# A gated state-space block with a ternary feed-forward: two convolutions moved from VectorE to TensorE, weight sums and step sizes rescheduled, and the first row of the tail in halves

## The reference, cut to what matters

```python
xi = in_proj_w @ ctx.T                      # 512 channels x 512 times
u  = silu(conv4(xi) + conv_b)               # depthwise, causal, 4 taps
dt_lo, Bm, Cm = split(x_proj_w @ u)         # 16, 16, 16 rows
delta = softplus(dt_proj_w @ dt_lo + dt_b)  # 512 x 512
state = state * exp(delta * A) + delta * u * B    # 16 states, scanned over time
y = sum_n(state * C) + D * u
y = y * silu(layernorm(x))                  # gate
x = x + tanh(g_xattn) * y.T
# then, on rows of x: ternary feed-forward
# s = mean|w|; wq = round(tanh(w / s)) * arctanh(s)      for w1, w2, w3 (2048 x 512)
# linear(v, w) = int8_round(rmsnorm(v)) @ wq
out = x + tanh(g_ffn) * linear(silu(linear(n, w1)) * linear(n, w2), w3),   n = layernorm(x)
```

## Time and profile before

| | us |
|---|---|
| median of 3 runs | 691.34 (689.88 to 695.04) |
| the profiled execution: its time | 689.91 |
| the profiled execution: its span | 687.9 |
| mean granted clock of PE | 0.928 |
| busy: PE / DVE / ACT / POOL | 605.1 / 609.2 / 557.1 / 550.8 |

### The profile page before, as it was taken

One profiled execution on the slowest core, in us unless ns is written; L12 is line 12 of the kernel. 1 busy time (PEld: TensorE's weight loads), 2 busy tenths in 40 slices (PEclk: granted clock), 3 DMA queues, 4 the chain that ended last, 5 costly groups with the idle time before them and its releaser, 6 DMA issues.

```text
span 687.9 us, 8231 instructions
## 1 busy us (share of the span) xinstructions
PE 605.1 (88%) x2538; PEld 247.5 (36%) x2538; DVE 609.2 (89%) x582; ACT 557.1 (81%) x804; POOL 550.8 (80%) x341
## 2 busy tenths in 40 slices
PE   6994657999788999999999999978898989787997
PEld 3430121445344343423333433332333333333443
DVE  4788889998897899999999999999999999977764
ACT  3648986588979998998989998989889878757883
POOL 5135548886987999999989999998999999978641
PEclk9857886999999999999999999999999999898999
DMA  7958963464953222215402212154212121000000
GB/s 206 331 149 275 331 220 122 135 201 134 281 204 89 46 62 54 84 48 126 100 24 61 49 53 55 50 123 108 62 46 55 38 55 40 15 16 0 22 28 30
DMA packets 40379, 70.97 MB, mean 103 GB/s; under 512 B 10848, under 2 KB 13408, under 8 KB 38288
## 3 DMA queue, kind: packets, MB, share of 16 engines
q1 hardware_dynamic: 32320, 48.44, 25.5%
q10 hardware_dynamic: 8016, 22.02, 9.5%
HBM read 49.46 MB, written 4.46 MB: 78 GB/s over the span
## 4 chain that ended last, share of the span: by engine, by line
PE 28%; DVE 23%; issue 7%; ACT 7%; POOL 4%; DVEq 0%; ACTq 0%; POOLq 0%
DVE hb L1201 14%; PE ring L1581 9%; DVE dbu_ps L1192 5%; PE y_ps L1559 5%; PE ring L1686 4%; PE du_ps L1546 3%; PE ring L1527 2%; POOL h L655 2%; ACT dA L918 2%; PE ring L1649 2%; DVE am L1260 1%; PE ring L1508 1%; PE ring L1641 1%; DVE h_max L1339 1%; POOL hb L712 1%
## 5 line engine op out<-in xcount | busy, mean ns | idle before, releaser
L1201 DVE TENSOR_TENSOR_SCAN hb<-dA,dbu_ps 128x1024 f32<-128x1024 f32 x128 | 292.1, 2282 | 11.0 <-ACT dA L918 4.3
L712 POOL TENSOR_TENSOR hb<-hb,bc_rep 128x2048 f32<-128x2048 f32 x52 | 236.0, 4539 | 38.4 <-DVE hb L1201 35.8
L1192 DVE TENSOR_TENSOR dbu_ps<-du_ps,bc_rep 128x1024 f32<-128x1024 f32 x128 | 157.8, 1233 | 19.5 <-PE du_ps L1546 10.5
L918 ACT ACTIVATE dA<-dl_rep,a_neg 128x511 f32<-128x511 f32 x252 | 160.8, 714 | 5.6 <-DVE hb L1201 3.5
L1559 PE MATMUL y_ps<-hb,sel_q 128*32 128x512 f32 x512 | 125.4, 635 | 1.3 <-POOL hb L712 1.2
L1546 PE MATMUL du_ps<-du,sel_q 32*128 32x512 f32 x128 | 77.1, 684 | 47.5 <-DVE dbu_ps L1192 44.5
L655 POOL TENSOR_TENSOR h<-h,up_sb 128x1024 f32<-128x1024 f32 x24 | 57.2, 2382 | 11.6 <-ACT up_sb L936 11.2
L1686 PE MATMUL ring<-w3T,hT 128*128 128x512 fp8e4 x256 | 61.2, 386 | 0.9 <-ACT hT L1007 0.5
L1559 PEld LDWEIGHTS y_ps<-hb,sel_q 128*32 128x32 f32 x512 | 28.6, 116 | 85.8 <-issue 81.8
L648 POOL TENSOR_TENSOR up_sb<-h,g3b 128x1024 f32<-128x1024 f32 x24 | 56.6, 2357 | 1.9
L1581 PE MATMUL ring<-w1T,a12T 128*128 128x512 fp8e4 x208 | 55.1, 389 | 1.2 <-ACT a12T L984 1.1
(11 more groups left out here) (182 smaller groups left out, 970.6 us busy)
## 6 DMA issues: line engine op xcount, KB each, us to landing
dl_rep<-delta SPq DMA_DIRECT2D x252, 64.0 KB, 2.0
bc_rep<-bc_scratch SPq DMA_DIRECT2D x28, 256.0 KB, 4.8
h<-in_L_ffn_w_dram ACTq DMA_DIRECT2D x7, 1024.0 KB, 5.8
x<-in_L_ffn_w_dram ACTq DMA_DIRECT2D x7, 1024.0 KB, 5.4
up_sb<-in_L_ffn_w_dram ACTq DMA_DIRECT2D x7, 1024.0 KB, 5.9
xt<-in_x_dram SPq DMA_DIRECT2D x16, 256.0 KB, 3.1
out_dram<-x SPq DMA_DIRECT2D x16, 256.0 KB, 2.0
x<-in_x_dram SPq DMA_DIRECT2D x2, 1024.0 KB, 8.2
```

The costliest lines, as they stand in the source:

```text
L712: g.tensor_tensor(hb[:, s % 4, :, :], hb[:, s % 4, :, :], c_rep(s // 16), ALU.mult)\
L918: ins = a.activation(dA[:, s % 2, i, 1:L], dl[:, 1:L], ACT.Exp, scale=a_neg[:, s % 16, i:i + 1])
L1192: v.tensor_tensor(dbu_ps[:, :, :], du_ps[:, :].unsqueeze(1).to_broadcast([P, 2, L]), b_rep(b)[:, 2 * half:2 * half + 2, :], ALU.mult).then ...
L1201: v.tensor_tensor_scan(hb[:, s % 4, 2 * half:2 * half + 2, :].rearrange("p a l -> p (a l)"), dA[:, s % 2, 2 * half:2 * half + 2, :].rearra ...
```

## The change

- The convolutions of tiles 4 and 5 go from DVE (steps 2 and 3) to PE, in step 1; ACT evacuates them in step 2. `tap` becomes a plain copy for them.
- The absolute sums of chunks 0 to 2 stand between the first `exps` of ACT, those of the chunks 3 to 11 in the steps 1 to 6. `exps(2)` stands ahead of ACT's loop. The refills are issued by SP (`next_chunk`) and not by ACT.
- The step sizes of step 0 are spread by DMA (`bcast_delta(0)`); L1621 goes. The load of the last z rows goes behind that of chunk 2.
- Three of the `z_row_stats` go ahead of step 0, and five stay, in the steps 4 to 8.
- `weight_scales` is split: `weight_sums` stays, the scales come after the second `add_input` of step 7, read the PSUM bank and have one instruction less.
- Tail: the row tile 12 is centred and gained by DVE in two halves (w1's row, w2's row), each with its own scale, quantisation, transpose and evacuation; PE gets ROW_FILL = 8 filling matmuls there. The statistics of rows 14 and 15 come later. The last states are summed in finer pieces. In row 15 all gains are on DVE, in three pieces, the sum of squares is in three, and LAST_FILL goes from 20 to 12.

```diff
-LAST_FILL = 20
+LAST_FILL = 12
+ROW_FILL = 8
...
 def late_convs(k):
+    if k == 0:
+        return [ET, AHEAD]
...
 def abs_chunks(s):
-    first = (0, 2, 4, 6, 8, 10, WCH)
-    return range(first[s], first[s + 1]) if s + 1 < len(first) else []
+    first = (3, 3, 4, 6, 7, 9, 10, WCH)
+    return range(first[s], first[s + 1]) if 0 <= s < len(first) - 1 else []
...  (SP)
-            for b in range(B):
+            for b in range(B - 1):
+                load_z(b)
...
+            def next_chunk(c):
+                sp.wait_ge(w_abs, c + 1)
+                load_chunk(c + WB)
...
             store_bc(0)
+            bcast_delta(0)
             bcast_delta(1)
             load_c(0)
             load_chunk(2)
+            load_z(B - 1)
...
+                    if s == 2:
+                        next_chunk(1)
+                    if s == 3:
+                        next_chunk(2)
+                    for c in abs_chunks(s - 2):
+                        next_chunk(c)
                     if s + 2 < Q * KQ:
                         bcast_delta(s + 2)
+                    if s == 1:
+                        next_chunk(0)
...  (POOL, after the loop)
-            row_rstd(TAIL)
-            row_rstd(TAIL + 1)
+            first_tail_powers()
             pool.wait_ge(a_tail, 2)
             times_up(TAIL - 1, 1)
-            row_rstd(TAIL + 2)
+            row_rstd(TAIL + 1)
             h_gain(TAIL - 1, 1)
-            row_rstd(TAIL + 3)
             hidden_rms(TAIL - 1)
             mul_gains(TAIL + 1)
+            row_rstd(TAIL + 2)
+            row_rstd(TAIL + 3)
...  (ACT)
+            def abs_sum(c):
+                act.wait_ge(*chunk_ld(c))
+                a.activation(chunk_buf(c), chunk_buf(c), ACT.Abs, accum_out=wsum[:, c:c + 1]).then_inc(w_abs, 1)
             exps(0)
             exps(1)
+            abs_sum(0)
             ctx_evac(1)
+            abs_sum(1)
+            exps(2)
             tap(ET)
+            abs_sum(2)
...
-                    elif 0 < s < Q * KQ - 1:
+                    elif 1 < s < Q * KQ - 1:
                         exps(s + 1)
...
+                    if q == (1 if k else 2):
                         for m in late_convs(k):
                             conv_evac(m)
...
                     for c in abs_chunks(s):
-                        act.wait_ge(*chunk_ld(c))
-                        a.activation(chunk_buf(c), chunk_buf(c), ACT.Abs, accum_out=wsum[:, c:c + 1])\
-                         .then_inc(w_abs, 1)
-                        act.wait_ge(w_abs, c + 1)
-                        a.dma_start(chunk_buf(c + WB), chunk_src((c + WB) % WCH)).then_inc(chunk_ld(c + WB)[0], 16)
+                        abs_sum(c)
...
-            square_sum(TAIL - 1, 0)
             quant(TAIL)
+            evac_first_aT(0)
+            evac_first_aT(1)
             normalise(TAIL + 1)
-            evac_aT(TAIL)
             square_sum(TAIL - 1, 1)
...  (DVE)
             copy_b(0)
+            z_row_stats(KQ // 2)
             copy_b(1)
+            z_row_stats(KQ // 2 + 1)
+            z_row_stats(KQ // 2 + 2)
...
+            def centred_gain(i):
+                v.scalar_tensor_tensor(a12[:, i, :], x1[:, (TAIL // ET) % XB, 0, :], fmv[:, TAIL % 4, 0:1],
+                                       (g2b if i else g1b)[:, :], ALU.subtract, ALU.mult).then_inc(a_tail, 1)
...
+            def weight_scales():
                 filled(dve, ("wsum", 0))
-                v.tensor_scalar(wm[:, :], bank(("wsum", 0))[:, 0:3], 1.0 / (H * D), None, ALU.mult).then_inc(w_mean, 1)
-                dve.wait_ge(w_mean, 1)
-                link(v.tensor_scalar(at[:, 0, :], wm[:, :], RMS_EPS, None, ALU.add))
-                link(v.tensor_scalar(at[:, 1, :], at[:, 0, :], 2 * ARTANH_HALF, None, ALU.mult))
+                total, mean = bank(("wsum", 0))[:, 0:3], 1.0 / (H * D)
+                v.tensor_scalar(wm[:, :], total, mean, None, ALU.mult).then_inc(w_mean, 1)
+                artanh = 2 * ARTANH_HALF
+                link(v.tensor_scalar(at[:, 1, :], total, artanh * mean, artanh * RMS_EPS, ALU.mult, ALU.add))
                 v.reciprocal(w_inv[:, :], at[:, 1, :]).then_inc(w_inv_done, 1)
-                link(v.tensor_scalar(at[:, 2, :], wm[:, :], -1.0, 1.0, ALU.mult, ALU.add))
+                link(v.tensor_scalar(at[:, 2, :], total, -mean, 1.0, ALU.mult, ALU.add))
                 link(v.reciprocal(at[:, 3, :], at[:, 2, :]))
-                v.scalar_tensor_tensor(at[:, 5, :], wm[:, :], 1.0, at[:, 3, :], ALU.add, ALU.mult).then_inc(w_scale, 1)
+                v.scalar_tensor_tensor(at[:, 5, :], total, float(H * D), at[:, 3, :], ALU.add, ALU.mult).then_inc(w_scale, 1)
...
                     add_input(s, 0)
-                    if k in (1, 2):
-                        z_row_stats(KQ // 2 + ET * (k - 1) + q)
-                    if k == 0 and q >= 2:
-                        convolve(ET + q - 2)
+                    if Q <= s < Q + 5:
+                        z_row_stats(KQ // 2 + 3 + s - Q)
                     if s == TERN_AT:
-                        weight_scales()
+                        weight_sums()
...
+                    if s == TERN_AT:
+                        weight_scales()
                     scan(s, 1)
...  (DVE, after the last scan)
             rows(TAIL)
-            row_bias(TAIL)
+            centred_gain(0)
+            first_tail_scale(0)
+            centred_gain(1)
+            first_tail_scale(1)
+            first_tail_dequant()
             rows(TAIL + 1)
-            tail_gains()
-            quant_scales(TAIL)
-            dequant_scales(TAIL)
+            hidden_max(TAIL - 1, 0)
             row_bias(TAIL + 1)
-            for ft in range(TAIL + 2, NT):
-                rows(ft)
-                row_bias(ft)
             for ft in range(TAIL, NT):
+                if ft == TAIL:
+                    mul_up(ft, 0)
                 hidden_row_scales(ft - 1)
-                mul_up(ft, 0)
+                if ft == TAIL:
+                    for late in (TAIL + 2, TAIL + 3):
+                        rows(late)
+                else:
+                    mul_up(ft, 0)
                 mul_up(ft, 1)
...
+                if ft == NT - 1:
+                    last_gain(0, 1024)
                 mul_up(ft, 2)
                 evac_hT(ft - 1)
...
+                if ft == NT - 1:
+                    last_gain(1024, 1536)
+                    hidden_max(ft, 0)
                 mul_up(ft, 3)
                 if ft == NT - 1:
-                    last_gain()
-                hidden_max(ft, 0)
+                    last_gain(1536, H)
+                else:
+                    hidden_max(ft, 0)
...  (PE, ahead of the loop)
-            pe.wait_ge(masks, 7)
-            pe.wait_ge(delta_done, 1)
-            mm(y_ps[:, :], sel_q[0:32, :], delta[0:32, 0, :], start=True, stop=True).then_inc(dl_bc, 1)
             bcast_du(0)
```

More of the change, by code:

```diff
@@ L1074, in _ @@
                             for c in range(4):
-                                if k == KQ - 1 and c == 3:
-                                    normalise(TAIL)
+                                if k == KQ - 1 and c == 2:
+                                    square_sum(TAIL - 1, 0)
                                 gate_silu(f, c)
@@ L1096, in _ @@
                 gate_silu(ft, 0)
[L1097 removed]
+                if TAIL < ft < NT - 2:
                     normalise(ft + 2)
@@ L1454, in _ @@
                     dequant_scales(ft + 1)
+                if ft == NT - 1:
+                    last_gain(0, 1024)
                 mul_up(ft, 2)
                 evac_hT(ft - 1)
+                if ft == TAIL:
+                    for late in (TAIL + 2, TAIL + 3):
+                        row_bias(late)
+                if ft == NT - 1:
+                    last_gain(1024, 1536)
+                    hidden_max(ft, 0)
                 mul_up(ft, 3)
                 if ft == NT - 1:
-                    last_gain()
-                hidden_max(ft, 0)
+                    last_gain(1536, H)
+                else:
+                    hidden_max(ft, 0)
                 if ft < NT - 1:
@@ L1561, in sum_states, with last_sums, state @@
                 ins.then_inc(sum_done, 1)
+            def last_sums():
+                s = Q * KQ - 1
+                def state(step, i):
+                    lo = 32 * (step % Q)
+                    return mm(y_ps[lo:lo + 32, :], sel_q[:, 0:32], hb[:, step % 4, i, :], start=False, stop=(i == NH - 1))
+                pe.wait_ge(hc_done, s)
+                state(s - 1, 0)
+                state(s - 1, 1)
+                pe.wait_ge(hc_first, 1)
+                for i in range(2):
+                    state(s, i)
+                    state(s - 1, 2 + i)
+                pe.wait_ge(hc_last, 1)
+                state(s, 2)
+                pe.wait_ge(hc_last, 2)
+                state(s, 3).then_inc(sum_done, 1)
             def skip_term(k):
@@ L1733, in _ @@
                     if q == 3:
+                        if f == 0:
```

(14 more changed lines are left out.)

158 lines of the change are left out of this document (97 added, 61 removed).

## The result

In the comparison made with the prediction, the changed kernel took 683.12 us (median of 4, 681.96 to 686.62), the kernel before 693.19 (4, 689.88 to 695.33): a ratio of 0.9889, interval 0.9855 to 0.9923. It is faster by a little over 1%, where 674.7 was forecast, in a range of 669 to 683: the median lies just above the range. Two later comparisons on other chips gave 682.88 against 690.84 (0.9902) and 684.62 against 693.06 (0.9895).

The account below looks back on a forecast made before the run. DVE's scans were taken as the backbone, with ACT bounding the head and PE's order the end. Gains of 14.0 (head), 0.8 (row 12) and 1.8 (row 15) sum to 16.6: span 671.3, median 674.7, range 669 to 683.

Parts of the forecast that it names:

- Rival A: Head: PE's convolutions run at the low clock, step 3 starts at 64.5, head gives 8; 681; chance 9%.
- rival B: Steps 8 to 19: late POOL or second-round loads hold PE's transposes, losing 4 to 8; 679 to 683; chance 14%.
- the head: Everything up to step 8: ACT's sums end at 92.8, step 8 begins at 100.2, 13.4 earlier.
- The tail: Behind the last scan: row 12 gains 0.8 and row 15 gains 1.8.
- The middle: Behind step 8: steps 9 to 11 save 1.6 in statistics, POOL's late product of step 7 costs 1.0.
- the wait is free: SP's refills ahead of each step's `bcast_delta`: waiting for a sum costs nothing while landings of up to 6.5 fit.
- Rival C: Step sizes queue behind chunk loads, `exps` of steps 3 to 9 late, about 4 a step; 700, slower; chance 4%.
- The start: Step 0: step sizes by DMA land near 32.2, `bcast_du(0)` ends sooner, step 0 begins at 33.2, 1.8 earlier.
- The scales: `weight_scales` before step 8: 7.4 where it was 11.9, with PE's sum over partitions hidden behind a scan.
- The port argument: Scales: DVE instructions with two SBUF inputs and POOL's exclude each other; reading PSUM shrinks those of 2.28 and 1.86.
- Row 12: Tail, row tile 12 in halves: `gate_up` starts near 621.7, `down(11)` at 635.1; gain 0.8, bounds -1 and 3.
- Row 15: Tail, last row tile: scales 1.1 earlier, 12 filling matmuls instead of 20; gain 1.8, bounds 1 and 2.5.

Follow-up runs that it names:

- the one with quarters: Kernel before, with each of the twelve second-round loads of weights cut to a quarter of its bytes; measured once, 685.98.
- the sizes first: Changed kernel with the step sizes of step 2 issued ahead of the loads of chunk 2 and the last z rows; 683.12 us.
- the z rows early: Changed kernel with the last batch's z rows loaded at the start, as before the change; 679.75 us, ratio to before 0.9841.
- all three: Changed kernel with z rows loaded at the start, row 12 as before, and step 2's step sizes ahead of chunk 2; 679.54 us, ratio 0.9817.

## Why the prediction was wrong

*Forecast 16.6 less; the medians differ by 8.0 to 10.1 in three comparisons.* Rival A had 681 and B 679 to 683, so the number alone would point near them. The table splits it. Three executions of before (the third is the one with quarters, whose head is the same: step 8 at 113.02) begin step 8 at 113.4 on average, three of the changed kernel at 106.7. By step 8 the head gave 6.6, not 13.4. The tail, from step 63 to the end, gave 1.0 to 1.2, not 2.6. The middle, forecast at 0.6, gave and took nothing that can be told from its own spread.

Step 8 was forecast at 100.2 and began at 106.7 on average. The 6.5 between them come from three pieces, of which the second is the large one. ACT's first decays began at 32.2 in the forecast and at 33.7 on average. From there to the end of ACT's sums the forecast had 60.6, and the three executions took 64.8 to 65.3; with the sizes first it was 64.3, with the z rows early 61.6, with both (all three) 61.1. From the sums to step 8 it was 8.0, not 7.4.

*The head: the landing of the step sizes of step 2.* This is the step of the prediction that failed. I took every landing of the four at up to 6.5, and wrote of the refills only that "the wait is free". The decays of step 2 were to end at 45.5; they began at 51.1, since three megabytes stood ahead in their queue. Rival C had this mechanism and this queue, and the sign it named, `exps` waiting for a DMA, is there. Its reach was wrong: it was priced for steps 3 to 9, at 4 a step, and nobody was late there, since SP issues those behind one refill with a step to spare. It bit once, in step 2, where the change itself had put the z rows. I never followed the move of `load_z(B - 1)` as an edit of its own: one line of the diff, costed at nothing without naming its cover. Undone, it gives 3.1 in the median and 3.3 at step 8 against the execution with the same fast start, so of the 4.4 lost up to the end of ACT's sums most is this one move. The Trainium skill (DMA: Bandwidth & Descriptors, "Queues, rings and completion order") says that a queue is consumed in ring order; by that the small DMAs come behind what is ahead of them. The traces agree: 2.1 with no load of 1 MB just ahead, 4.7 behind 1 MB, 7.3 behind 2, 9.2 behind 3.

*The rest of the head.* From step 3 to step 7 the forecast had 31.7 and the changed kernel took 31.74. I had written that a wait of over 5 before step 3 means rival A, the low clock. It was 5.45, but most of it was not the clock. PE waited 3.6 for the tap, and 1.5 came with it: the sixteen pieces ran 8.58 and not 7.11, with a granted clock of 1.00 before the pause and of 0.61 just behind it. With the z rows early 1.72 of the wait stays, the 1.7 of the forecast. The windows (columns as in rows 1):

```profile
49.00:53.00 4.00, 1.58 (x4) 0.30 (x2) 3.11 (x3) 1.91 (x4) 2.58 (x1) 1.00 1.05 325
54.20:58.00 3.80, 3.80 (x6) 1.78 (x7) 3.66 (x3) 3.80 (x4) 0.73 (x1) 0.61 1.04 310
```

With the z rows early the pause was 0.3, the granted clock 1.00 from 49 to 56, and nothing was lost. The start gave 0.1 to 0.5 in two executions and 2.8 in the third, not 1.8: it goes with the pace of the sixteen `in_proj` matmuls, as said above, and where it came out better than forecast that is luck. The scales: from the weight sum to step 8 7.9 (8.3 in the second execution), forecast 7.4. The port argument was right, in form and in sign: the small instruction with two SBUF inputs, put back, ended with POOL's rounding again.

*The middle (rival B).* After the first pair of traces it looked as if the middle had taken back 4.2. The second execution of before refuted this. The first one of before had passed steps 13 to 21 faster than all others with whole loads. The part of B that POOL causes is real but small. The forecast charged 1.0 for it, which makes 39.8 from step 8 to step 13 (before took 40.4). The executions that had waited 1.3 to 1.8 for `bcast_du(8)` took 39.6 to 39.8, those that had waited 0.2 to 0.5 took 41.3 to 41.6 (the kernel with the scales as before, without any wait there, 40.3): the 1.5 is paid on one side of step 8 or the other.

*Row 12.* This term failed too, in size and sign, by less. Forecast 0.8 earlier, measured 0.5 to 0.8 later. `gate_up(12)` did start 2.7 earlier relative to the last sums (619.66 against 607.26, and 624.52 against 609.46 before). It then ran into hidden 11, as forecast. Counted from the last sums, the scales of hidden 11 came 0.6 later than forecast (626.84 - 607.26 = 19.6, not 628.4 - 609.46 = 18.9), and the end of `mul_up(12, 2)` 0.4 (24.7, not 24.3); from there to `down(11)` it was 2.5 and not 1.3. PE of the changed kernel:

```profile
628.08 0.62 PE L1757 MATMUL ring<-ident,up_sb 128*128 128x128 f16 x8 [1.88 <-ACT up_sb L1034]
629.68 0.61 PE L1757 MATMUL ring<-ident,up_sb 128*128 128x128 f16 x8 [0.97 <-DVE hb L1287]
630.12 1.43 PE L1700 MATMUL ring<-w1T,a12T 128*128 128x512 fp8e4 x4
632.08 1.89 PE L1700 MATMUL ring<-w2T,a12T 128*128 128x512 fp8e4 x4 [0.52 <-DVE hb L1287]
```

The transposes come in two halves with a hole between, `mul_up(12, 1)` frees the bank late behind the two deferred statistics, and the last four matmuls take 1.89, those at 624.3 and 625.2 1.02 and 1.03: the low clock, avoided at the start of the row, comes back at its end (granted 0.50 from 632 to 634). In the kernel with the convolutions on DVE the same four took 1.04 at a granted clock of 1.00, and `down(11)` came 33.9 behind step 63, not 34.9. So the clock is up to 1 of it, and not in every execution. That is the bound of -1 that I had given, and not the value I took.

*Row 15.* 1.8 forecast, 1.8 measured: from the filling matmuls to the end it is 12.6 in both executions of before and 10.8 to 10.9 in the three of the changed kernel.

## What to carry to other kernels

Follow every DMA that a diff moves, however small its line, and add up the bytes ahead of each small transfer in the same queue; a landing time is a property of the queue at that moment, not of the transfer. When a wait for data is shortened by reordering one queue, look at who stands behind: here reordering gave 1.0 up to the end of ACT's sums, and a megabyte taken out of the queue 3.7. And before a stage is said to give back a gain, take a second profile of the kernel before: here the first one got 5.3 ahead of the next in one stage, with the same program.

## What the runs showed that I had not expected

With the same program the first sixteen `in_proj` matmuls take 7.13 or about 9 to 10, at a granted clock that reads 1.00 in both cases; step 0 moved by up to 2.7 with it in the changed kernel, and by 0.1 in before. In steps 14 to 21, where DVE and POOL wait for the B and C rows and the DMA share reaches 1.0 for ten us, the same program took 61.9 and 65.5 in two executions of before, and 63.6 to 68.2 in those of the changed kernel and its variants; with a quarter of the bytes 60.0 and 61.5.
